# The second half's encoder laid beside the first half's top-k turns, and the experts of all groups beside the second half's

## The reference

```
x = x + encoder(layernorm(x))             # 4 layers: linear attention, 16 heads of 8, and a feed-forward 128-512-128
x = x + cross_attention(layernorm(x), ctx, mask)        # 16 heads, softmax
x = x + quantized_ffn(layernorm(x))       # 8-bit activations, ternary weights, depthwise convolution of 3 taps
x = x + topk_attention(layernorm(x))      # each query keeps its 64 best of 128 keys, per head
x = x + channel_attention(layernorm(x), ctx)            # attention between channels, 4 heads of 32, twice
n = layernorm(x)
x = x + sum over 8 experts: (silu(n @ Wg) * (n @ Wu)) @ Wd      # every token through all experts
```

```
scores = einsum('bhqd,bhkd->bhqk', q, k) / sqrt(8)
_, idx = top_k(scores, 64)
attn   = softmax(where(in idx, scores, -inf)) @ v
```

## Time and profile before

| | us |
|---|---|
| median of 3 runs | 1564.43 (1564.06 to 1566.5) |
| the profiled execution | 1569.24 |
| its span, first to last instruction | 1567.3 |
| PE busy (share) | 1097.3 (70%) |
| DVE busy | 1014.1 (65%) |
| ACT busy | 723.6 (46%) |
| POOL busy | 451.3 (29%) |
| mean granted clock of PE | 0.78 |

### The profile page before, as it was taken

How to read it: one execution, slowest core, us unless ns; L and a number is a source line. 1 busy time by engine, 2 the same in 40 slices (tenths; PEclk the granted TensorE clock), 3 DMA queues, 4 the chain that set the end, 5 groups by cost and what they waited for, 6 DMA issues and landing times. The chain is left out here.

```text
span 1567.3 us, 17720 instructions
## 1 busy us (share of the span) xinstructions
PE 1097.3 (70%) x4778; PEld 658.2 (42%) x4778; DVE 1014.1 (65%) x3150; ACT 723.6 (46%) x2072; POOL 451.3 (29%) x430
## 2 busy tenths in 40 slices
PE   3888746645787756645236756997889739898788
PEld 2666613323676623323023533443444315454333
DVE  6565686687666676686668885568747686544222
ACT  2443438532444428634735545656546535233111
POOL 4322334203333324302624353224313332201000
PEclk9898957657998966756555556998879968799899
DMA  4101100000100000000000000111011100111121
GB/s 155 28 27 27 26 28 1 1 0 0 28 26 12 24 25 1 1 1 0 1 0 1 1 8 1 41 41 41 21 55 41 41 21 21 55 61 57 38 74 47
DMA packets 35415, 42.20 MB, mean 27 GB/s; under 512 B 5680, under 2 KB 20288, under 8 KB 35328
## 3 DMA queue, kind: packets, MB, share of 16 engines
q1 hardware_dynamic: 34656, 39.27, 8.2%
q0 software_dynamic: 672, 1.98, 0.4%
HBM read 40.18 MB, written 1.05 MB: 26 GB/s over the span
## 5 line engine op out<-in xcount | busy, mean ns | idle before, releaser
L1576 DVE TENSOR_TENSOR big<-psum,qe 128x512 f32<-128x512 f32 x128 | 87.9, 687 | 225.0 <-PE psum L1125 108.2
L802 ACT ACTIVATE qe<-psum 128x512 f32<-128x512 f32 x128 | 75.0, 596 | 225.1 <-PE psum L1116 224.9
L1106 PE MATMUL psum<-big,wd 128*128 128x512 f32 x256 | 139.0, 628 | 0.0
L744 ACT ACTIVATE far<-far,half_far,fmul 128x128 bf16<-128x128 bf16 x256 | 102.9, 482 | 54.6 <-DVE hit L1363 54.6
L1293 DVE TENSOR_SCALAR h<-xs,mv,rstd 128x128 f32<-128x128 f32 x192 | 79.6, 477 | 66.4 <-POOL rstd L502 66.4
L500 POOL TENSOR_SCALAR veps<-mv 128x4 f32<-128x4 f32 x52 | 12.3, 236 | 378.5 <-DVE mv L1286 378.5
L701 ACT ACTIVATE Wk<-S,nsm 128x128 f32<-128x128 f32 x256 | 98.7, 387 | 16.1 <-DVE nsm L1720 16.1
L1376 DVE MAX8 near<-Wk 128x8 f32<-128x128 f32 x512 | 103.4, 277 | 0.7
L1015 PE MATMUL psum<-ctxT,kT 32*128 32x512 f32 x128 | 48.9, 845 | 73.0 <-DVEq L1452 41.4
L1038 PEld LDWEIGHTS psum<-vaug,big 128*128 128x128 f32 x512 | 88.6, 259 | 20.0 <-issue 19.9
L889 PE MATMUL psum<-ident,h 128*128 128x128 f32 x176 | 36.6, 328 | 86.2 <-DVE h L1293 73.1
(11 more groups left out here) (259 smaller groups left out, 2690.0 us busy)
## 6 DMA issues: line engine op xcount, KB each, us to landing
wg<-in_mg SPq DMA_DIRECT2D x32, 256.0 KB, 2.7
wu<-in_mu SPq DMA_DIRECT2D x32, 256.0 KB, 3.0
wd<-in_md SPq DMA_DIRECT2D x32, 256.0 KB, 3.6
w<-in_aw SPq DMA_DIRECT2D x9, 256.0 KB, 3.1
w<-in_w2a SPq DMA_DIRECT2D x9, 256.0 KB, 2.6
ctxt<-in_ctx SPq DMA_DIRECT2D x8, 256.0 KB, 3.8
wqkv<-in_aw SPq DMA_DIRECT2D x9, 192.0 KB, 2.3
rowkv<-in_arow SPq DMA_DIRECT2D x9, 128.0 KB, 3.0
```

Source lines behind the costliest of these rows:

```text
L744: ins = act.activation(far[t][:, hd, :], far[t][:, hd, :], ACT.Identity, bias=half_far[:, 0:1], scale=fmul[t][:, hd:hd + 1])
L802: act.activation(sg[k % 2], bank(5 + k % 2), ACT.Silu).then_inc(silu_done, 1)
L1106: pe.matmul(bank(4), wd[e % 2][:, c, :], hid[k % CH], start=(k % NCHUNK == 0), stop=(k % NCHUNK == NCHUNK - 1), skip_group_check=True).the ...
L1576: dve.tensor_tensor(hid[k % CH], bank(U_BANK[k]), sg[k % 2], ALU.mult).then_inc(hu_done, 1)
```

## The change

**Order.** The encoder loop runs for the first half only. After the first half's cross attention and projections comes `beside_encoder`: points -12 to 119, that is turns -1 to 9, with the top-k of sequences 0 to 7 alone, and in the same points the second half's encoder in steps. A step is one layer for one slot (four sequences); there are `STEPS = 8`. Turn `b` issues `attend(b+1, p)` (norm's transposes to the residual after the output product) and `feed(b, p)` (hidden layer to the next norm), both in forms of 512 columns, in banks 3 to 7. The weights of the second half's layers are loaded by a plain loop on SP.

**Second stage of points.** Then the second half's cross attention, feed-forward and projections run as before, and then the points from 84 (turn 7) to the end, with the top-k of sequences 8 to 15. Here the channel attentions start at points 84, 102, 166 and 214 (before at 70, 118, 166, 214), and chunks are issued at nine points of a turn: 90 in turns 8 to 17, 38 behind them. The attention outputs of groups 0 and 1 are turned, projected and added within `beside_encoder` (`attended_turned`, `attended_projected`, `attended_added`).

**Buffers.** In the first stage of points the exponentials, the turned maxima and the attention output lie in the experts' weight tiles, so the first experts are loaded only when `at_mm` has counted 2, instead of at the start. Counts of semaphores are worked out from the order (`norm_no`, `turned_no`, `up_no`, `NX_AT`).

The core of the diff:

```diff
-FIRST = 5 * PTS + 10
-GROUP = G * PTS
+RANGES = ((0, NB), (NB, NSEQ))
+START2 = (NB - 1) * PTS
+CH_START = (START2, START2 + 18, (2 * G + 5) * PTS + 10 + (G - 4) * PTS, (3 * G + 5) * PTS + 10 + (G - 4) * PTS)
-CHUNK_PTS = (0, 1, 3, 4, 6, 7, 9, 10)
+CHUNK_PTS = (0, 1, 3, 4, 5, 6, 7, 9, 10)
+STEPS = SLOTS * L
...
+            sp.wait_ge(at_mm, 2)
+            for k in range(2):
+                load_expert(k, k)
...
+            def encoder(t, p):                       # POOL
+                if 0 <= t < STEPS:
+                    attend(t, p)
+                if 1 <= t <= STEPS:
+                    feed(t - 1, p)
...
+            def beside_encoder():                    # ACT
+                for t in range(-PTS, (NB + 2) * PTS):
+                    b, p = t // PTS, t % PTS
+                    topk(b, p, 0)
+                    if 0 <= b + 1 < STEPS:
+                        attend(b + 1, p)
+                    if 0 <= b < STEPS:
+                        feed(b, p)
...
+            def attend(k, p):                        # PE
+                if p == 0:
+                    pe.wait_ge(ln_h, 2 * norm_no("A", k)[0])
+                    transposes(bank(4), h[s], ident[:, :], hT_mm, 2)
+                if p == 1:
+                    pe.wait_ge(hT_done, turned_no("A", k))
+                    for b in range(G):
+                        mm = pe.matmul(pair[:, b, :], hT[s][:, b * P:(b + 1) * P], wqkv[:, P:3 * P], start=True, stop=True)
+                    pe.matmul(bank(5), wqkv[:, 0:P], hT[s][:, :], start=True, stop=True).then_inc(q_mm, 2)
...
+            def feed(k, p):                          # PE
+                if p == 1:
+                    transposes(bank(6), h[s], ident[:, :], hT_mm, 2)
+                if p in (2, 3):
+                    for c in (2 * p - 4, 2 * p - 3):
+                        pe.matmul(bank(7 - c % 2), w1[:, c * P:(c + 1) * P], hT[s][:, :], start=True, stop=True).then_inc(w1_mm, 2)
+                if p == 5:
+                    for b in range(G):
+                        for c in range(CH):
+                            mm = pe.matmul(bank4(7)[:, b, :], big[s][:, c, b * P:(b + 1) * P], w2[:, c, :], start=(c == 0), stop=(c == CH - 1))
...
+            def attend(k, p):                        # DVE, points 2, 3, 4, 6, 8, 11
+                if p == 3:
+                    dve.wait_ge(q_exp, both(s, i + 1))
+                    dve.scalar_tensor_tensor(qT_of[1][s][:, :], qe[s][:, :], 1.0, qT_of[1][s][:, :], ALU.min, ALU.add).then_inc(q_pos, 2)
+            def feed(k, p):                          # DVE
+                if p == 0:
+                    step_normalize("F", k)
+                if p == 6:
+                    dve.tensor_tensor(xs_of[1][s][:, :, :], bank4(7), xb[s][:, :, :], ALU.add).then_inc(x_upd, 2)
+                    step_norm("A", k + 2)
+                if p == 8:
+                    step_normalize("A", k + 2)
...
+            encode_half()                            # every engine
+            cross_and_forward(0)
+            beside_encoder()
+            cross_and_forward(1)
+            for t in range(START2, LAST_POINT):
+                if t < TURNS * PTS:
+                    topk(t // PTS, t % PTS, 1)
                 for g in range(NG):
-                    channel(g, t - FIRST - GROUP * g)
+                    channel(g, t - CH_START[g])
```

More of the change, by code:

```diff
@@ L76, with enc_orders @@
 TINY = float(2.0 ** -100)
+STEPS = SLOTS * L
+def enc_orders():
+    norms, turned = [("A", 0), ("A", 1)], []
+    for t in range(STEPS + 1):
+        if t < STEPS:
+            turned.append(("A", t))
+        if t >= 1:
+            turned.append(("F", t - 1))
+            norms.append(("A", t + 1))
+        if t < STEPS:
+            norms.append(("F", t))
+    return {e: j for j, e in enumerate(norms)}, {e: j for j, e in enumerate(turned)}
+NORM_AT, TURNED_AT = enc_orders()
+NX_AT = {}
+for _e in [("project", 0), ("project", 1)] + [(w, g) for g in range(NG) for w in (("project",) if g > 1 else ()) + ("stats1", "add", "stats2")]:
+    NX_AT[_e] = len(NX_AT) + 1
 def chunk_points():
@@ L125, with channels_by, results_by, last_u_in_3 @@
 U_BANK, U_PREV = u_banks()
-Y_AT = [CHUNK_AT[NCHUNK * g + NCHUNK + LAG - 1] if g + 1 < NG else CHUNK_AT[-1] + LAG for g in range(NG)]
+def channels_by(t):
+    return sum(c < t for c in CH_START)
+def results_by(t):
+    return sum(y + 1 < t for y in Y_AT)
+def last_u_in_3(t):
+    return max([k for k in range(len(CHUNK_AT)) if U_BANK[k] == 3 and CHUNK_AT[k] <= t], default=None)
 def decoder(nc, x, ctx, mask, aw, acolA, acolB, arow, w2a, bw, bcol, brow, cw, cconv, dw, dcol, drow,
@@ L427, in _ @@
                 load_ctx(s, s * G)
-            for k in range(2):
-                load_expert(k, k)
-            for hf in range(HALVES):
+            for hf in range(1):
                 with sp.Fori(0, L) as l:
@@ L774, in channel, with beside_encoder @@
+            def beside_encoder():
+                for t in range(-PTS, (NB + 2) * PTS):
+                    b, p = t // PTS, t % PTS
[4 more added lines that the diff above has]
+                        feed(b, p)
+                    if p == 10 and b in (5, 9):
+                        attended_out(b // G - 1, 6)
             def channel(g, r):
-                if r == 0:
-                    act.wait_ge(at_mm, g + 1)
-                    act.copy(attT[:, :], bank(3)).then_inc(at_out, 1)
+                if r == 0 and g > 1:
+                    attended_out(g, 3)
@@ L810, in _, with encode_half @@
             act.wait_ge(preset, 1)
-            for hf in range(HALVES):
+            def encode_half():
+                hf = 0
                 qT, kT = qT_of[hf], kT_of[hf]
@@ L874, in _ @@
                     projected(s, hf)
-            for t in range(-PTS, LAST_POINT):
+            encode_half()
+            cross_and_forward(0)
+            beside_encoder()
+            cross_and_forward(1)
+            for t in range(START2, LAST_POINT):
                 if t < TURNS * PTS:
-                    topk(t // PTS, t % PTS)
+                    topk(t // PTS, t % PTS, 1)
                 for g in range(NG):
-                    channel(g, t - FIRST - GROUP * g)
+                    channel(g, t - CH_START[g])
                 for k in GATES_OF.get(t, ()):
@@ new lines, in beside_encoder @@
+            def beside_encoder():
+                for t in range(-PTS, (NB + 2) * PTS):
+                    b, p = t // PTS, t % PTS
+                    topk(b, p, 0)
+                    if 0 <= b + 1 < STEPS:
+                        attend(b + 1, p)
+                    if b == 6 and p == 2:
+                        pe.wait_ge(n_x, NX_AT["project", 0])
+                    if 0 <= b < STEPS:
+                        feed(b, p)
+                    if p == 10 and b in (5, 9):
+                        attended_turned(b // G - 1, 6)
+                    if p == 11 and b in (5, 9):
+                        if b < STEPS:
+                            pe.wait_ge(x_upd, 2 * norm_no("A", b + 2)[1])
+                        attended_projected(b // G - 1, 7)
@@ L1468, in head_outputs, with topk @@
                                   zden[a % 2][:, :].unsqueeze(2).to_broadcast([P, H, DH]), ALU.mult).then_inc(po_done, 1)
-            def topk(b, p):
-                short = 0 <= b - 1 < NSEQ
-                if p == 0 and 0 <= b < NSEQ:
+            def topk(b, p, half):
+                lo, hi = RANGES[half]
+                short = lo <= b - 1 < hi
+                if p == 0 and lo <= b < hi:
                     sides(b)
@@ L1617, in _, with embed @@
                 normalize(s, LN_IN, xin[s])
[L1618 to L1619 removed]
+            def embed(hf):
+                half_now[0] = hf
                 n0 = hf * NLN
@@ new lines, in beside_encoder, with encode_half @@
+            def beside_encoder():
+                for t in range(-PTS, (NB + 2) * PTS):
+                    b, p = t // PTS, t % PTS
+                    topk(b, p, 0)
+                    if b == 6 and p == 0:
+                        attended_added(0, 7)
+                    if 0 <= b + 1 < STEPS:
+                        attend(b + 1, p)
+                    if 0 <= b < STEPS:
+                        feed(b, p)
+                attended_added(1, 7)
+            def encode_half():
+                hf, n0 = 0, 0
```

416 lines of the change are left out of this document (324 added, 92 removed).

## The result

Slightly slower. The changed kernel takes 1571.9 us (median of 12 runs, 1564.8 to 1579.0) against 1566.9 (1564.1 to 1570.9) for the kernel before beside it: ratio 1.0034, 95% interval 1.0018 to 1.0050. I had forecast 1556 and called faster likelier than slower (0.48 to 0.45). The profiled execution has a span of 1572.7 us against 1567.3.

The account below looks back on a forecast made before the run. No single engine bounds it: PE and DVE alternate in the encoder, DVE sets plain top-k turns, PE those with experts. 387.9 + 414 + 174.8 + 582 = 1558.7, less 2.9, gives 1556 us; range 1525 to 1605.

Parts of the forecast that it names:

- turns 8 and 9 of the second stage: Second top-k stage, turns with light top-k and channel attention 1: 31 and 39 us.
- turns 0 and 1: First top-k stage, turn 0 without short list and turn 1 without turned scores: 32 and 40 us.
- Turns 13 and 14: Second top-k stage, turn 13 with the other exact selection 61.5 us, turn 14 bound by DVE 54 us.
- the result's turn: Second top-k stage, turn 12 with group 0's result: 46 us, from 46.67 less 0.7.
- the tail: Work after the last turn, nearly all PE: loses a chunk, 140.6 us against 143.24 before.
- the forecast's case: Whole kernel with merged turns of 45 us: 1556 us, own range 1535 to 1580, chance 0.42.
- rival 3: Merged turns' chain of waits longer than laid out: turns of 50 us, +28, 1584 us in all; chance 0.23.
- The merged turn: First top-k stage, top-k with an attention and a feed-forward step: 45 us each, ends 40 and 52.
- queue-order sum: Merged turn's DVE work of 31 us plus 10.4 of waits and stretch: 41.4 at full clock, 46.4 starting at half.
- Rival 1: PE at full clock through merged turns: 41.4 to 40 us each, -26, 1530 us in all; chance 0.20.
- Rival 2: PE at half clock through up- and down-products too, becoming the bound: turns of 54 us, +55, 1611 us; chance 0.15.
- eats most of the 168: Double fill and drain, about 68 us, and merged turns' extra 18 us each use up most of the encoder's 168.42.

Follow-up runs that it names:

- e4: Changed kernel plus 26 unused identity products on PE in each merged turn's gaps, to raise its clock: 1567.2 us, ratio 1.0006 to the kernel before.
- e2: Changed kernel with ACT's copy of the feed-forward's transposes moved behind the second score exponential and last penalties: 1559.1 us, ratio 0.9953 to the kernel before.
- e6: Changed kernel with channel attention 1 of the first half started four points earlier: 1570.4 us, ratio 1.0037 to the kernel before.
- e7: Changed kernel with eight expert chunks a turn instead of nine: 1571.7 us, ratio 1.0060 to the kernel before.
- e5: Changed kernel with the merge alone undone, top-k turns first, then the encoder steps alone: 1636.3 us, ratio 1.0471 to the kernel before.
- e12: e9 plus the earlier start of channel attention 1 from e6: 1518.0 us, ratio 0.9694 to the kernel before.
- e1: Changed kernel with POOL issuing the feed-forward's rstd ahead of its top-k multiplication in merged turns: 1573.0 us, ratio 1.0046 to the kernel before.
- e9: Changed kernel with e2's copy move, DVE steps later, K/V and Q products earlier on PE, ACT reordered: 1525.1 us, ratio 0.9736 to the kernel before.

## Why the prediction was right or wrong

**The sign was wrong, and the sum was 14 us short.** It stood at 1558.7 of span; 1572.7 was measured. Two steps failed. I gave the second channel attention no term for its waits, where it is a chain through three queues (turns 8 and 9 of the second stage, +15.1 us). And I priced turns with little top-k by their work, where their waits stay (turns 0 and 1, +6.5). Turns 13 and 14 add 4.1 and turns 15 to 17 3.6; the result's turn took 9.1 less and the tail 5.0 less than I had, and all other terms come to -1.2 together. The measured time lies in my range, between the forecast's case and rival 3's, but partly by luck: two misses of the opposite sign took 14 us off.

**The merged turn: right.** 45 forecast, 45.2 on average over turns 3 to 6. The queue-order sum (41.4 at full clock, 46.4 with the half-clock start) and its waits, one by one, are in the trace: rstd 4.38 (I had 4.4), queries 2.75 (1.8), the stretched instruction 3.50 (3.5), the down product 3.90 (0.7). The 5 us that I added for the clock in one lump show up in the last wait and the one for the queries (+4.2 us). I had put them down to the half-clock start; e4 shows that the start alone is worth little, and its turn 6 points to the clock in the middle of the turn. Turn 2 had 67.6 us against 67, turn 7 36.7 against 35, the drain 39.7 against 40, the cross stage 174.6 against 174.8.

**Turns 0 and 1: +6.5 us.** I took 32 and 40 by leaving the missing top-k work out. But a merged turn is a chain of waits, and these stay when the work between them goes: turn 0 has DVE busy 19.54 of 35.43 us, with 5.0 us waited for rstd, 3.8 for the queries and 4.2 at the down residual: 15.9 us not busy, more than the 12.1 of turn 4. e2, which shortens the two latter, brings turn 0 to 32.3. The step that failed is pricing a light turn by its work.

**Turns 8 and 9 of the second stage: +15 us**, the largest miss (35.8 and 49.3 against 31 and 39). I wrote "light top-k and channel 1", charged the channel attention at its PE work and put its waits at nothing, without a row for that. The rows of before had its price: the turn with one takes 15.4 us more than a plain turn with the same eight chunks (51.42 against 36.03). e6 shows that the price goes with the channel attention, and the timeline above through which queues. Turns 13 and 14 were near (63.4 and 56.3 against 61.5 and 54), turn 7 had 26.0 against 27.5.

**The result's turn: 9 us less than I had.** I took turn 12 of before, 46.67 us, as the price of group 0's result. In the trace of before ACT's copy of that result stood between the two score exponentials and waited 3.18 us for the lagging down product; the second exponential, the penalties, a table load of 1.28 and the silu stood behind it, DVE waited 10.8 us for the silu and PE 5.76 for DVE. With nine chunks a turn the last chunk of the group comes at the end of turn 11, and the copy waits for nothing that is late:

```profile
1163.51 0.58 ACT L977 ACTIVATE qe<-psum 128x512 f32<-128x512 f32 x1
1164.33 0.59 ACT L983 COPY ctxt<-psum 128x512 f32<-128x512 f32 x1 [0.25 <-PE psum L1382]
```

Turn 11 has 39.3 us with it and turn 12 has 36.95. In e7, where the copy comes in the middle of turn 12 and waits 1.11 us, that turn has 41.6 us. Over a plain turn of the same kernel the result costs 10.6 us in before, about 6.7 in e7 and 2.2 in the changed kernel: most of the price was the place in the turn.

**The tail** gained what I said and more (135.6 us against 140.6), and turns 15 to 17 gave 3.6 of it back (109.9 against 106.3).

**Rival 1 (full clock, -26 us)** did not come about: turns 3 to 6 have a mean granted clock of 0.68 to 0.78. Its price was sound where the clock came near it: turn 6 of e4, at 0.92, took 41.2 us, and rival 1 had 40 to 41.4. No run held the changed kernel's turns there, so what full clock throughout would give is not shown. **Rival 2 (half clock, PE bound)** didn't either: PE is busy for 34.8 of the 46.5 us of turn 4, and DVE's waits and stretched instructions set the turn. **Rival 3** was right in kind for the turns at the stage's ends, not for the merged ones.

**What my sum did not see at all** is that it was a difference of large terms. I gave the double filling and draining and the merged turns' extra 18 us as what "eats most of the 168". e5 shows what stands behind it: the overlap as written brings 60 us, and 49 of them are spent on cutting the encoder into steps of four sequences. (In e12 the first stage is 109 us under e5's, 480.6 - 371.9, but the order of e12 was never run apart, so not all of that need be overlap.) With a price for the step alone (23.7 us of one chain's latency, measured in e5, against the 21 of an eighth of the encoder) this trade would have stood beside the sum as a check. A forecast of 0.5% that is the difference of such terms carries hardly any knowledge of the sign.

What stays open: what makes the clock go one way or the other through the same instructions (42.2 or 45.8 us in turn 3), and whether this explains all of the changed kernel's spread, 1564.8 to 1579.0. Only single executions were profiled. Nor was turn 8 run without a channel attention in it, so its 4.8 us over my 31 are not divided between the channel and the light turn.

## What to carry to other kernels

Before two stages are laid on each other, price each alone in the form that the merge needs; the form can cost most of what the overlap brings. When they are merged by hand, the order inside each engine's queue decides what the merge is worth: here the merge as written lost 5 us, and moving a handful of steps and one channel attention's start (e12) took 54 off it. Removing DVE's largest wait alone brought nothing (e1), so move to the next row of the same engine's timeline and ask what that one would meet, above all which POOL instruction it would run beside.

## What the hardware showed that I had not expected

- A DVE instruction of 0.34 us with a single SBUF tensor as input (a `tensor_scalar` of 128x128 float32) took 3.52 us beside POOL's 3.60 us one. I had expected this only of instructions with two SBUF inputs, as the earlier trace rows showed it. MAX8 and MATCH_REPLACE8 beside the same POOL instructions kept their 0.27.
- It goes the other way as well. In e9 POOL's addition of 128x4, 0.23 us in the changed kernel, took 2.06 while DVE marked the dropped keys, an instruction with two SBUF inputs:

```profile
596.75 2.26 DVE L1711 TENSOR_TENSOR drop<-S,theta 128x2048 bf16<-128x2048 f32 x1
```
```profile
597.03 2.06 POOL L724 TENSOR_SCALAR veps<-mv 128x4 f32<-128x4 f32 x1 [10.05 <-DVE mv L1949]
```

- The same instructions of turn 3 took 42.2 us in one execution and 45.8 in another. The granted clock was 0.50 in the first nine us of both; in the third it was 1.00 in one and 0.74 in the other.
